# State space kernel: GpSimd forms three of the sixteen products with B instead of two, in place over the spread rows

## The reference

```python
conv = conv_b + sum(xp[k:k + L] * conv_w[:, k] for k in range(4))
xc = silu(conv)
dbc = xc @ x_proj_w.T                    # 4 columns dt, 16 of B, 16 of C
delta = softplus(dt @ dt_proj_w.T + dt_proj_b)
A = -exp(A_log)
h = h * exp(d[:, None] * A) + (d * xt)[:, None] * b[None, :]     # for each pixel in turn
y = h @ c + xc * D
y = y * silu(z)                          # then a projection, a normalisation, silu, and a residual
```

## Time and profile before

| What | Value |
|---|---|
| Median of three runs | 12469.56 us (12467.69 to 12474.12) |
| The profiled execution's own time | 12465.74 us |
| Its span, first to last instruction | 12463.9 us |
| PE busy | 11440.9 us (92%) |
| DVE busy | 9896.2 us (79%) |
| ACT busy | 7888.2 us (63%) |
| POOL busy | 7860.5 us (63%) |
| DMA, all queues | 1433.35 MB |

### The profile page before, as it was taken

One profiled execution on the slowest core, in us unless ns is written; L12 is line 12 of the kernel. 1 busy time (PEld: TensorE's weight loads), 2 busy tenths in 40 slices (PEclk: granted clock), 3 DMA queues, 4 the chain that ended last, 5 costly groups with the idle time before them and its releaser, 6 DMA issues.

```text
span 12463.9 us, 161217 instructions
## 1 busy us (share of the span) xinstructions
PE 11440.9 (92%) x33768; PEld 4251.5 (34%) x33768; DVE 9896.2 (79%) x12696; ACT 7888.2 (63%) x12821; POOL 7860.5 (63%) x5925
## 2 busy tenths in 40 slices
PE   4989898989899999999999999999999999999998
PEld 1333333333333333333333333333333333333333
DVE  6454545454536344999999999999999999999999
ACT  2333333333333334888888888888888888888888
POOL 6030303030303001999999999999999999999999
PEclk9989898989899999999999999999999999999999
DMA  2010101010100001444444444444444444444444
GB/s 59 2 29 2 28 2 29 2 28 2 29 9 21 3 1 52 174 185 173 180 184 171 183 181 173 185 178 176 185 174 179 185 171 183 182 172 185 179 175 186
DMA packets 408439, 1433.35 MB, mean 115 GB/s; under 512 B 180242, under 2 KB 180370, under 8 KB 267926
## 3 DMA queue, kind: packets, MB, share of 16 engines
q1 hardware_dynamic: 408342, 1432.48, 30.9%
HBM read 1380.68 MB, written 51.62 MB: 115 GB/s over the span
## 4 chain that ended last, share of the span: by engine, by line
DVE 22%; issue 22%; PE 7%; ACT 4%; POOL 3%; DVEq 2%; POOLq 0%; ACTq 0%; DMA 0%; SPq 0%
DVE bbank L940 10%; DVE h L961 9%; POOL e L837 3%; PE vbank L1144 2%; PE vbank L1143 2%; PE ybank L1195 2%; DVE qn L930 1%; ACT L1018 1%; ACT sz L1015 1%; PE ubank L1147 1%; PE bbank L1185 1%; ACT da L1085 1%; ACT so L1053 1%; DVE dl L919 1%; DVE yb L926 1%
## 5 line engine op out<-in xcount | busy, mean ns | idle before, releaser
L871 POOL TENSOR_TENSOR pr<-h,cc 128x512 f32<-128x512 f32 x4109 | 5157.1, 1271 | 543.8 <-DVE h L961 543.6
L961 DVE TENSOR_TENSOR_SCAN h<-da,h,bbank 128x512 f32<-128x512 f32 x3596 | 4497.4, 1261 | 0.0
L1195 PE MATMUL ybank<-pr,m_small 128*128 128x512 f32 x8212 | 4141.5, 595 | 0.3 <-POOL pr L871 0.3
L433 ACT ACTIVATE prob<-st 128x512 f32<-128x512 f32 x2048 | 1222.7, 597 | 2573.5 <-PE st L565 2573.5
L1085 ACT ACTIVATE da<-dl,a 128x512 f32<-128x512 f32 x3599 | 2445.4, 713 | 148.4 <-DVE dl L919 138.4
L940 DVE TENSOR_TENSOR bbank<-bbank,du 128x512 f32<-128x512 f32 x3597 | 2415.7, 672 | 4.4 <-POOL du L841 2.1
L308 DVE TENSOR_REDUCE mpart<-s 128x1 f32<-128x512 f32 x2048 | 1321.4, 686 | 1089.7 <-PE s L531 1081.6
L565 PE MATMUL st<-qf,kf 65*128 (+1 forms) x4096 | 2121.1, 620 | 5.9 <-ACT qf L437 5.9
L241 POOL TENSOR_TENSOR rowsum<-xin 128x1024 f32<-128x1024 f32 x64 | 154.0, 2406 | 2994.2 <-PE vb L598 2905.9
L1185 PE MATMUL bbank<-bcs,selb 96*128 96x512 bf16 x3598 | 1387.3, 386 | 474.4 <-DVE h L961 464.2
L1195 PEld LDWEIGHTS ybank<-pr,m_small 128*128 128x128 f32 x8212 | 1519.4, 191 | 829.7 <-POOL pr L871 378.5
(11 more groups left out here) (156 smaller groups left out, 12201.2 us busy)
## 6 DMA issues: line engine op xcount, KB each, us to landing
cc<-c_rows SPq DMA_DIRECT2D x1032, 1024.0 KB, 8.0
cc<-c_rows SPq DMA_DIRECT2D x258, 512.0 KB, 11.5
upw<-up SPq DMA_DIRECT2D x260, 256.0 KB, 10.3
xin<-x SPq DMA_DIRECT2D x128, 512.0 KB, 6.7
out<-ot SPq DMA_DIRECT2D x256, 128.0 KB, 2.3
zw<-zn_tokens SPq DMA_DIRECT2D x780, 32.0 KB, 10.5
c_rows<-crows SPq DMA_DIRECT2D x258, 36.0 KB
zn_tokens<-znb SPq DMA_DIRECT2D x64, 128.0 KB, 2.0
```

The costliest lines, as they stand in the source:

```text
L433: act.activation(prob[t % 4][:, :], st[t % 2][:, :], ACT.Exp).then_inc(exp_done, 1)
L871: pool.tensor_tensor(pr[:, n % 8, :], h[:, n, :], cc[par][:, n, :], ALU.mult).then_inc(prod_done, 1)
L961: dve.tensor_tensor_scan(h[:, n, :], decay, inp, h[:, n, TB - 1:TB], ALU.mult, ALU.add).then_inc(scan_done, 1)
L1195: pe.matmul(ybank[:, :], w("ident"), pr[:, n % 8, :], start=False, stop=(n == S - 1))\
```

## The change

`POOL_B` gets state 13 as a third. So DVE no longer multiplies it by `du`, PE no longer spreads its row of B, and ACT writes its decay in step 13 into PSUM, not in step 9 into the ring. POOL gets its product in front of step 6; the one of state 10 stays at step 2 and that of state 15 at step 10. The tile `dbp` is gone: POOL writes the products over the spread rows of B in `cc[par]`, and the scan reads them there. As this tile exists once for each parity, POOL's wait for the scan of the tile before falls away, and SP waits, before it loads new rows of B, for all scans of the tile that last used them (it has just waited for all products of that tile). The transfer of the rows of B has three rows.

```diff
-POOL_B = (10, 15)
-AT_STEP = {2: 0, 10: 1}
+POOL_B = (10, 13, 15)
+AT_STEP = {2: 0, 6: 1, 10: 2}
...
-        dbp = sb("dbp", [P, NB, TB])
...
                 if not first:
-                    sp.wait_ge(dbp_done, (tau - 1) * NB)
+                    sp.wait_ge(scan_done, (tau - 1) * S)
                 sp.dma_start(cc[par][:, S:S + NB, :].rearrange("p n t -> p (n t)"),
...
                 pool.wait_ge(b_in[par], count * 16)
-                if not first:
-                    pool.wait_ge(scan_done, (g - 1) * S + POOL_B[k] + 1)
-                pool.tensor_tensor(dbp[:, k, :], cc[par][:, S + k, :], du[par][:, :], ALU.mult).then_inc(dbp_done, 1)
+                pool.tensor_tensor(cc[par][:, S + k, :], cc[par][:, S + k, :], du[par][:, :], ALU.mult)\
+                    .then_inc(dbp_done, 1)
...
                 if n in POOL_B:
-                    decay, inp = bbank[n % 4][:, :], dbp[:, POOL_B.index(n), :]
+                    decay, inp = bbank[n % 4][:, :], cc[par][:, S + POOL_B.index(n), :]
```

## The result

The changed kernel takes 12653.38 us (median of 4 runs, 12650.01 to 12655.84) against 12468.76 us for the kernel before (median of 4 runs too), a ratio of 1.0147 with a 95% interval of 1.0129 to 1.0165. The forecast was 12648. The profiled execution spans 12651.0 us.

The account below looks back on a forecast made before the run. A loop over DVE and POOL, within 0.1 us of DVE's own work, bounded the kernel. The new loop of 29.99 us against 29.29 gives +0.70 per tile, x 256 = +179 us: forecast 12648 us, range 12585 to 12695.

Parts of the forecast that it names:

- The loop: DVE tile opening to state 4's scan 10.06, to POOL's product 1.42, 14 POOL instructions to du 17.20, back 1.31: 29.99 us.
- P7's 0.27 us: Wait of POOL's product with C of state 7 for its scan, expected to disappear in the added product.
- P4's 0.96: Wait in us of POOL's product with C of state 4 for its scan, ahead of the added product; expected to remain.
- DVE's saving at nothing: DVE's own work falls 0.60 us to 28.38 per tile, but it then waits 1.6 us for du.
- In place, waits, transfer: In-place writing and dropped POOL wait cost or give nothing; SP's 768 KB transfer lands in time, even 5.8 us later.
- The stall: DVE's wait in each second tile for ACT's decay of state 10, late by 0.44 us; forecast to end.
- M0: DVE's product that opens a tile, state 0's product with du; forecast to wait 1.6 us per tile for du.
- A: Rival: DVE sets the time, POOL's 2.1 us of idle swallow the product; -233 us, 12237 us; chance 0.07.
- B: Rival: POOL's idle before its state 4 product is usable, du keeps its place; -64 us, 12406; chance 0.03.
- C: Rival: POOL's added instruction holds up DVE, 29.61 us per tile; +82 us, 12552 us; chance 0.02.
- D: Rival: no change beyond 0.2%, the loop being some 0.6 us shorter than summed; chance 0.03.
- E: Rival: slower still, dl late too or the larger transfer late; each 0.1 us is 26 us; chance 0.02.

Follow-up runs that it names:

- unused product: The kernel before plus one POOL product of 128x512 into a tile nobody reads: 12655.27 us at step 6, 12470.36 us at step 3.
- the fastest version: The changed kernel with both moves, state 13's product at step 3 instead of 6 and du behind the product of step 11: 12240.9 us, ratio 0.9817.
- The run with the convolution first: The changed kernel with du two instructions earlier, and PE's convolution and gate products at step 0 ahead of adding state 13's product: 12276.07 us, ratio 0.9843.

## Why the prediction was right

**The loop.** Each of the four terms came within 0.02 us. The step that decided was to ask not how idle POOL was but which of its idle times lay behind the added product and ahead of `du`. At step 6 that is only P7's 0.27 us; P4's 0.96 lies ahead of the product and can't take it up. At step 3 it is both, 1.23 us, just the length of the product. The pair of runs with the unused product shows this step by itself, 12655 against 12470 us.

**DVE's saving at nothing.** Right: the run without it takes the same time. DVE's wait for du was 1.5 to 1.6 us per tile as forecast. One sum of the range is off by 4 us and changes nothing: 0.87 x 256 above 12469.56 is 12692, not 12696.

**In place, waits, transfer.** Right, at nothing, by the run with that part alone. This covers the waits and the writing; the third row's transfer was not taken alone, but between 5104 and 12600 us no wait of POOL for the rows of B is listed in the changed kernel, and the fastest version carries it too. Of its 768 KB the prediction feared up to 5.8 us more to landing; in the changed kernel it landed 12.2 us after its issue (median from 9000 to 9600 us), where 512 KB took 11.5 in the kernel before.

**ACT.** The stall went as forecast, and the reason given holds: with one decay fewer ahead of it, ACT's way from the silu `xc` to the decay of state 10 takes 12.83 us in the tile that used to stall, instead of 13.45, so 0.62 us less where 0.68 was priced. The run with the unused product at step 6 bears it out: there M0 waits for `du` too, but ACT's list is the old one, and the stall stays. But it ended with only 0.08 us to spare (decay at 9065.64, 0.80 more to the earliest scan, scan at 9066.52), which the prediction did not work out. It took the start of ACT's chain as fixed, and this start hangs on PE and through it on POOL's P13. In the tiles that stall the convolution starts 3.03 us behind M0 before the change and in the changed kernel, 3.43 with du one instruction forward and 3.76 with two, while the way from `xc` on stays at 12.83 us; so the stall came back in these two runs. The run with the convolution first shows the dependence itself.

Why only each second tile stalls is to be seen in the kernel before:

```profile
9008.52 1.28 ACT L1010 ACT_TABLE_LOAD   x1 [3.72 <-PE vbank L1144]
...
9034.42 1.28 ACT L1010 ACT_TABLE_LOAD   x1
```

In the tile that stalls, ACT changes its function table for the silu (1.28 us) only once the convolution is there, and `xc` starts 3.33 us behind the start of the convolution (9006.49 to 9009.82). In the other tile the table is changed ahead of the convolution, and it is 1.91 us (9036.00 to 9037.91). The changed kernel has the same two distances. What sets the two places of the table load apart was not looked into.

**The rivals.** A, with DVE setting the time at 12237 us, was wrong for this kernel but gave the time of the version with both moves, 12241. Its condition was du by 27.07 us after M0, and moving two instructions met it. The Trainium skill's rule (Perfetto Trace Analysis, section Identifying the Most-Contended Engine), to work first on the engine with the highest occupancy, agrees with that version's trace, where DVE is busy 1000 of 1000 us and its own work is the period. In the changed kernel DVE is the fullest engine too, at 950, but there the rule leads astray: the run with the unused product at step 6 gives DVE a product more and takes the same time. B fell with P4's wait of 0.94 us still there, and du 28.67 us behind M0, not 27.7. C fell with both engines full in the same stretch and DVE's scans at 1268 ns in the group of the changed kernel, and D and E had no sign in the trace.

## What to carry to other kernels

Idle time on the engine that takes over work counts only if it lies behind the place of the added work and ahead of the result that the other engine waits for; idle time ahead of that place can't take it up. Write down the stretch from the last release from outside to that result, count the instructions in it, and close the loop. If two limits lie within 0.1 us of each other before a change, relieving one alone gives next to nothing, and the place of a single added instruction can decide the sign: 1.5% slower at step 6, 0.3% faster at step 3, and 1.8% faster with du one instruction earlier as well. After opening a loop, look for what now comes late, measured from the new start of the tile, on the third engine too.

## What the runs showed of the hardware

The write of the C and B rows to DRAM has 19 rows of 2 KB instead of 18, 36 to 38 KB, and SP's wait for it more than doubled. The view lists SP's waits in two rows of about half the tiles each. The first row of the kernel after:

```profile
SPq L783 <- DMA c_rows<-crows: 384.7, 128, 3.0
```

The second has 337.8 us in 130 times. In the kernel before they are 163.8 us in 128 times and 122.7 in 130. So SP waits 3.01 us instead of 1.28 for a transfer of the same queue, and 2.60 instead of 0.94. All five kernels with 18 rows have the short waits (163.8 to 172.2 us in the first row), and all seven kernels with 19 have the long ones. It was hidden in all of them: no wait of POOL for the spread rows is listed in any. Why one row more costs 1.7 us was not looked into.
